# Attention: the low half of one key projection copied behind the maxima of the next unit

## The reference, cut to what matters

```python
x = x + 0.5 * _L0_ffn_ref(_layernorm(x), ...)
x = x + _L0_attn_ref(_layernorm(x), ...)
x = x + 0.5 * _L0_ffn_ref(_layernorm(x), ...)
x = x + 0.5 * _L1_ffn_ref(_layernorm(x), ...)
x = x + _L1_attn_ref(_layernorm(x), ...)
x = x + 0.5 * _L1_ffn_ref(_layernorm(x), ...)

def _L1_attn_ref(x, Wq, bq, Wk, bk, Wv, bv, Wo, bo):     # 16 heads of 16
    q = split_heads(x @ Wq + bq)
    k = split_heads(x @ Wk + bk)
    v = split_heads(x @ Wv + bv)
    attn = jnp.einsum('bhqd,bhkd->bhqk', q, k) / jnp.sqrt(jnp.float32(HEAD_DIM))
    attn = jnp.where(causal, attn + alibi, jnp.finfo(jnp.float32).min)
    p = jax.nn.softmax(attn, axis=-1)
    out = jnp.einsum('bhqk,bhkd->bhqd', p, v).transpose(0, 2, 1, 3).reshape(Bx, Tx, C)
    return out @ Wo + bo
```

## Time and profile before

| What | Value |
|---|---|
| Median of 3 runs | 1861.5 us (1861.46 to 1861.55) |
| The profiled execution's own time | 1860.93 us |
| Its span, first to last instruction | 1858.7 us |
| PE busy, of the span | 1801.2 us (97%) |
| DVE busy | 1331.0 us |
| ACT busy | 950.1 us |
| POOL busy | 583.9 us |
| Mean granted TensorE clock, of full speed | 0.997 |

### The profile page before, as it was taken

One profiled execution on the slowest core, in us unless ns is written; L12 is line 12 of the kernel. 1 busy time (PEld: TensorE's weight loads), 2 busy tenths in 40 slices (PEclk: granted clock), 3 DMA queues, 4 the chain that ended last, 5 costly groups with the idle time before them and its releaser, 6 DMA issues.

```text
span 1858.7 us, 26733 instructions
## 1 busy us (share of the span) xinstructions
PE 1801.2 (97%) x9607; PEld 1383.5 (74%) x9607; DVE 1331.0 (72%) x1867; ACT 950.1 (51%) x1806; POOL 583.9 (31%) x402
## 2 busy tenths in 40 slices
PE   8999999999999999998799999999999999999999
PEld 6888888888454545534578888888888886777888
DVE  6666666567899999999966666565676556777533
ACT  4442323333688768787645433233334337898422
POOL 1000243100488879888730000000000025655000
PEclk9999999999999999999999999999999999999999
DMA  5332335221122222223202233232221306663100
GB/s 201 88 96 71 98 121 164 65 61 35 58 74 69 74 80 75 74 68 116 81 18 81 71 98 104 65 107 64 62 73 56 66 1 121 119 133 71 38 12 23
DMA packets 84203, 146.41 MB, mean 79 GB/s; under 512 B 13864, under 2 KB 23720, under 8 KB 83560
## 3 DMA queue, kind: packets, MB, share of 16 engines
q1 hardware_dynamic: 84072, 144.72, 27.5%
HBM read 130.38 MB, written 14.29 MB: 78 GB/s over the span
## 4 chain that ended last, share of the span: by engine, by line
PE 76%; DVE 12%; issue 5%; ACT 4%; POOL 2%; DMA 0%; SPq 0%; DVEq 0%; POOLq 0%; ACTq 0%
PE psum L161 20%; PE psum L162 19%; PE psum L163 19%; PE psum L1557 6%; DVE scan_state L1757 5%; PE psum L1410 2%; PE psum L2169 2%; POOL scan_state L1258 1%; ACT attn_p L2317 1%; PE psum L278 1%; DVE moe_hidden_lo L866 1%; PE psum L1508 1%; PE psum L2121 1%; ACT attn_p L2311 1%; PE psum L1531 1%
## 5 line engine op out<-in xcount | busy, mean ns | idle before, releaser
L793 ACT ACTIVATE moe_hidden_hi<-moe_hidden 128x512 fp32r<-128x512 f32 x200 | 126.3, 631 | 399.2 <-DVE moe_hidden L846 398.2
L1258 POOL TENSOR_TENSOR scan_state<-scan_delta_u,scan_B_rows 128x1024 f32<-128x1024 f32 x127 | 299.3, 2367 | 81.3 <-PE psum L1557 58.2
L161 PE MATMUL psum<-xnT_hi,moe_w_hi 128*128 128x512 f32 x800 | 315.5, 394 | 0.5 <-DVE xnT_lo L475 0.2
L162 PE MATMUL psum<-xnT_lo,moe_w_hi 128*128 128x512 f32 x800 | 313.6, 392 | 0.0
L163 PE MATMUL psum<-xnT_hi,moe_w_lo 128*128 128x512 f32 x800 | 311.4, 389 | 0.0
L1757 DVE TENSOR_TENSOR_SCAN scan_state<-psum,scan_state 128x1024 f32<-128x1024 f32 x128 | 291.5, 2282 | 0.4
L842 DVE TENSOR_TENSOR moe_gated_up<-moe_gate_rows,psum 128x512 f32<-128x512 f32 x184 | 126.5, 688 | 210.1 <-PE psum L163 128.5
L423 POOL TENSOR_SCALAR rstd<-mean_var 128x2 f32<-128x2 f32 x48 | 10.6, 222 | 718.0 <-DVE mean_var L457 717.9
L161 PE MATMUL psum<-moe_w_hi,moe_hidden_hi 128*128 128x256 f32 x800 | 230.2, 288 | 3.6 <-DVE moe_hidden_lo L866 2.2
L1557 PE MATMUL psum<-scan_state,ident 128*128 128x512 f32 x480 | 226.8, 595 | 2.2 <-DVE scan_gated L1772 1.4
L163 PE MATMUL psum<-moe_w_hi,moe_hidden_lo 128*128 128x256 f32 x800 | 226.2, 283 | 0.0
(11 more groups left out here) (238 smaller groups left out, 3520.6 us busy)
## 6 DMA issues: line engine op xcount, KB each, us to landing
scan_B_rows<-scan_B SPq DMA_DIRECT2D x127, 256.0 KB, 3.2
moe_gate_rows<-gate_table SPq DMA_DIRECT2D x176, 128.0 KB, 3.0
moe_w_raw<-moe_pack SPq DMA_DIRECT2D x50, 384.0 KB, 4.0
attn_stack<-attn_rows SPq DMA_DIRECT2D x96, 128.0 KB, 5.5
moe_gate_rows<-gate_table SPq DMA_DIRECT2D x32, 224.0 KB, 3.0
ffn_w_raw<-ffn_pack SPq DMA_DIRECT2D x16, 384.0 KB, 4.0
moe_gate_rows<-gate_table SPq DMA_DIRECT2D x32, 160.0 KB, 2.7
moe_gate_rows<-gate_table SPq DMA_DIRECT2D x24, 192.0 KB, 2.9
```

Of the source, the lines that this page charges most:

```text
L161: e.matmul(out, wH, xH, start=start, stop=False)
L162: e.matmul(out, wH, xL, start=False, stop=False)
L793: e.activation(self.hH[:, b, :], self.hb[:, b, :], ACT.Copy).then_inc(self.s_hH.sem, 1)
L1258: e.tensor_tensor(self.st[q % self.NBUF][:], self.dtu[:, 2 * h:2 * h + 2, :], self.Bs[:, q % self.RING, :].unsqueeze(1).broadcast_to([P, 2 ...
```

## The change

VectorE's copy of the low rows of `k0` moves from the end of the pass u = 2 to the pass u = 3, behind the two maxima (`first` and `second`) of that pass. It is the same instruction on the same data. There are three such copies, in chunks 0, 1 and 2; chunk 3 has no chunk behind it.

```diff
                 first(n + 2)
             if n + 2 < self.N:
                 second(n + 2)
+            if u == 3:
+                job(c, 2, 1)
             norm(c, u)
             job(c, u, 0)
             keep(n)
             if n and n % 2 == 0:
                 out_lo(n // 2 - 1)
-            job(c, u, 1)
+            if u != 2:
+                job(c, u, 1)
```

## The result

| | Before | After |
|---|---|---|
| Median of 6 runs each, us | 1861.52 (1861.36 to 1862.34) | 1869.33 (1867.96 to 1870.74) |
| The profiled execution, us | 1860.93 | 1869.35 |
| Its span, us | 1858.7 | 1867.2 |

The changed kernel takes 1.0041 times as long (95% interval 1.0031 to 1.0051), 7.8 us more. The direction was forecast, the size was not: 1865.8 us was predicted, and 1869.33 lies above the range.

What follows compares the result with a forecast made beforehand. PE was taken as the bound, 76% of the chain that ended last. Delays of 1.51 + 0.95 + 1.80 = 4.26 us at units 8, 16 and 24, added to the median, gave 1865.8 us; range 1863.4 to 1867.4.

Steps and rivals of the forecast that it cites:

- The path: At three places the copy starts 1.80 us later, so the batches do too, and PE waits at units 8, 16, 24.
- TensorE's next job: Same bank, needs the copy: hardly 0.1 us late, covered by a wait of 0.43 us; taken as zero.
- The gain at the seam: First maximum and exponentials up to 0.66 us earlier, at most 1.3 us in all; lost in batch waits, taken as zero.
- The waits: Scores of units 8, 16 and 24 start later by 1.51, 0.95 and 1.80 us, 4.26 us in all.
- the bounds of the batches: All three batches taking 12.7 us would lose 2.7 us in all; all taking 13.5 us, 5.1 us.
- the clock: Rival: PE idles over 2 us at unit 8, and one further clock fall costs 1.3 us and more: 1867.2 us, chance 0.12.
- The fall spared near 1704: Rival: shifted waits near 1704 spare the clock fall already there, giving 1864.4 us; chance 0.13.
- Hidden: Rival: PE waits for something else by the time the batch lands, so no change, 1861.5 us; chance 0.04.
- The fit: A 128 KB transfer takes 2.3 us, so the batch lands near 1574, 6 us to spare, and the sum is zero.
- the faster rival: Each batch lands before PE comes to it, so 3 x 0.43 = 1.3 us is gained: 1860.2 us; chance 0.03.
- Nothing before it changed: The stretch from 1536 to the attention's end grows 4.3 us, and everything ahead of it keeps its time.

Runs made afterwards that it cites:

- sp_late: Kernel before, VectorE's order unchanged, but SP holds each next chunk's first key rows until VectorE's second maximum of the next unit is done: 1869.4 us, 1.0038.
- after_split: Changed kernel, but SP sends six query transfers of the first half of chunks 1 to 3 before it waits for the key rows: 1860.74 us, 0.9995.
- keep_busy: Changed kernel, but PE makes seven extra masking products before it waits for the batch at units 8, 16 and 24: 1865.81 us, 1.0022.
- split_all: after_split, with the query transfers sent first in chunk 0 as well, for both `kb`: 1861.69 us, 1.0001.
- split_busy_end: after_split, with four extra masking products before the scores of units 28 and 31: 1860.9 us, 0.9992.
- only_c0: Changed kernel, but with the copy moved in chunk 0 alone: 1863.53 us, 1.0011.
- only_c1: Changed kernel, but with the copy moved in chunk 1 alone: 1864.05 us, 1.0014.

## Why the prediction was right, and where it failed

*The path.* Right in every step: the copy 1.81 us late (1.80), the first maximum and ScalarE's wait as said, TensorE's next job 0.1 us late under a wait that covers it, the first issues of the batches later by as much as the copy, PE waiting for them at all three units. The gain at the seam comes and is lost in the waits, as said. `sp_late` shows that the late batch alone is enough for the loss, `after_split` that with an early batch nothing of it is left.

*The waits.* 4.41 us against 4.26, and the terms are off by just what the batches were off. Batches 1 and 3 took 13.1 us instead of 13.5, and units 8 and 24 lost 1.10 and 1.39 instead of 1.51 and 1.80: 0.4 less each. Batch 2 took 13.6 instead of 12.7, and unit 16 lost 1.92 instead of 0.95, idling 2.66 us instead of 1.2. Both ends stood in the bounds of the batches; the value taken for each, its own row, was the wrong choice: the same batch takes another time in each execution (the first 12.4 to 13.5 us, the second 12.7 to 13.6, the third 11.8 to 13.5 in the seven profiles that send it whole). That the errors nearly cancel is luck, and so are the idle times at units 8 and 24, 2.30 and 2.13 us as said: the batches were 0.4 us quicker, and PE came 0.4 us earlier by its gain at the seam.

*The step that failed: the clock.* It stood among the rivals as one further fall of 1.3 us and a little more, with a chance of 0.12. The profiled execution has two, 1.61 and 1.53 us, and `keep_busy` gives 3.5 us back by median. The price of one was right within 0.3 us; the chance was wrong, and so was the number of falls. The argument against it was that waits near 1690 had left the clock at 1.00. But these were of some 1 us each in the matmuls' rows (1.40 before unit 28's scores in those of the weight loads), and the prediction itself made waits of 2.3 and 2.1 us by the weight loads; the one fall that the trace before did show in the attention stood behind 1.18 us (1.50 by the weight loads). A wait that the change creates at three places is three tries, not one: with two falls at the 1.3 us that the earlier trace rows gave, the sum would have been 1861.5 + 4.26 + 2.6 = 1868.4.

*Rivals.* The fall spared near 1704 did not come: the window 1712 to 1716 of the changed kernel, 8 us later, has it at 0.75. Its price was wrong too: `split_all` and `split_busy_end` have no such fall and gain nothing by that, since PE waits for VectorE's copy behind it. Hidden is excluded by the three waits. The fit of "DMA: Bandwidth & Descriptors" of the Trainium skill ("Anatomy of one DMA — SWDGE (gpsimd) path"), which would have hidden the delay, is not borne out here: the last transfers took 8.0, 7.0 and 7.2 us from issue to landing, not the estimate of 2.3 us worked out from it; as the prediction says, it is given for another issuing path. The gain of the faster rival is real (0.31 to 0.37 us at a seam, not 0.43), and it stays only where the batch is early, as that rival said: `after_split`.

*"Nothing before it changed"* was off by 1.17 us between the two profiled executions, that of before being 0.6 us under its median. What lies behind the first seam, 4.41 + 3.14 - 0.34 = 7.2 us, accounts for all but 0.6 of the 7.8 us between the medians; where that 0.6 is was not settled.

## What to carry to other kernels

Before moving a small copy later, follow it through the queue that it feeds: here 1.8 us on an engine with time to spare held up two row transfers and twelve more that took 13 us, and PE met their end. When a change makes TensorE idle, count the idle time and then look for what it does to the granted clock behind it, once for each place; filling the wait with products whose result is thrown away tells the two apart. Where one late input holds back a whole batch, send the part that does not need it ahead, but only if most of it drains before the late part comes.

## What was unexpected of the hardware

Idle times of the same length were not always followed by a fall of the clock: 2.30 us at unit 8 of the changed kernel was, 2.66 at its unit 16 was not, 2.30 in `only_c0` and 2.27 in `only_c1` were not, 1.95 in `sp_late` was; 1.18 us by the matmuls' rows before unit 31's scores was in the kernel before, and was not in `split_all`. What decides it was not found. The spread of the runs does not tell it either: the changed kernel's lie 2.8 us apart, those of the kernel before 1.0 beside it but 2.6 to 3.2 beside the experiments. A fall can also cost nothing, as near 1705, where PE has a later wait that takes it up. And a batch of twelve transfers for units 8, 16 and 24 took 11.8 to 13.6 us in the seven profiles that send it whole. The transfers behind it on SP wait for it: in the kernel before, the next query rows were issued at 1572.18 and landed at 1580.5, right behind the batch at 1580.1, and in `split_all` it took 5.4 us (1552.60 - 1547.17) from the issue of the key rows to the start of the transfers that need them.
